# Moving score chunks and mixes among the projections of an attention body

## The reference

```python
q = _split_qk(x @ Wq.T, b, n) * SCALE
k = _split_qk(x @ Wk.T, b, n)
v = (x @ Wv.T).reshape(b, n, H, 2 * D).transpose(0, 2, 1, 3)
att = jnp.einsum('bnqd,bnkd->bnqk', q, k)
att = jax.nn.softmax(att.astype(jnp.float32), axis=-1)
diff = att[:, :, :H, :H] - lam * att[:, :, H:, H:]
out = jnp.einsum('bnah,bhnd->bnad', diff, v)
out = out * jax.lax.rsqrt(jnp.mean(out * out, axis=-1, keepdims=True) + EPS)
out = out * (1.0 - LAM_INIT)
return out.reshape(b, n, DIM) @ Wo.T + bo
```

## Time and profile before

| what | value |
|---|---|
| median of 3 runs | 1276.65 us (1274.16 to 1279.75) |
| the profiled execution | 1274.55 us, its span 1272.7 us |
| TensorE busy | 1100.6 us, 86% |
| VectorE busy | 939.4 us, 74% |
| ScalarE busy | 587.1 us, 46% |
| GpSimd busy | 205.9 us, 16% |
| first `xtl` of body 4 and of body 5 | at 258.81 and 324.28 us |

### The profile page before, as it was taken

How to read it: one execution, slowest core, us unless ns; L and a number is a source line. 1 busy time by engine, 2 the same in 40 slices (tenths; PEclk the granted TensorE clock), 3 DMA queues, 4 the chain that set the end, 5 groups by cost and what they waited for, 6 DMA issues and landing times.

```text
span 1272.7 us, 22077 instructions
## 1 busy us (share of the span) xinstructions
PE 1100.6 (86%) x7424; PEld 873.7 (69%) x7424; DVE 939.4 (74%) x1932; ACT 587.1 (46%) x906; POOL 205.9 (16%) x202
## 2 busy tenths in 40 slices
PE   5988989889797979635599998998989989899995
PEld 4766767667575757424378787787877878778784
DVE  4287878787878888786858677696785867958746
ACT  4333333333243333310346555566555655655683
POOL 3100030303131312132140103003030030210000
PEclk9999999999898989767599999999999999999998
DMA  7566475766657565983530021201211012100001
GB/s 278 158 175 160 140 163 174 157 186 137 200 120 221 100 183 117 290 215 113 193 100 34 1 67 67 66 10 56 66 66 53 13 66 66 66 1 2 34 1 66
DMA packets 184334, 139.32 MB, mean 109 GB/s; under 512 B 140128, under 2 KB 152416, under 8 KB 180192
## 3 DMA queue, kind: packets, MB, share of 16 engines
q1 hardware_dynamic: 113120, 113.57, 31.8%
q10 hardware_dynamic: 71168, 25.17, 8.2%
HBM read 82.09 MB, written 52.43 MB: 106 GB/s over the span
## 4 chain that ended last, share of the span: by engine, by line
PE 66%; DVE 9%; ACT 7%; issue 7%; SPq 5%; DMA 4%; POOL 1%; ACTq 0%; DVEq 0%; POOLq 0%
PE ps_f L558 18%; PE ps_s L744 14%; PE ps_f L728 12%; PE ps_s L577 9%; PE ps_o L679 6%; DMA qbd<-q_scr 3%; SPq L382 3%; PE ps_o L597 2%; ACT h_sb L947 2%; DVE h_acc L1279 1%; ACT r_sb L941 1%; PE ps_t L619 1%; PE ps_f L679 1%; DMA w_raw<-in_L_attn_Wv 1%; ACT oth L919 1%
## 5 line engine op out<-in xcount | busy, mean ns | idle before, releaser
L728 PE MATMUL ps_f<-x2h,w 128*128 128x512 f32 x512 | 204.7, 400 | 1.6 <-DVE x2l L1260 1.6
L744 PE MATMUL ps_s<-w,hh 128*128 128x512 f32 x500 | 201.5, 403 | 0.0
L728 PE MATMUL ps_f<-x2l,w 128*128 128x512 f32 x512 | 200.7, 392 | 0.0
L744 PE MATMUL ps_s<-w,hl 128*128 128x512 f32 x500 | 199.3, 399 | 0.0
L1268 DVE TENSOR_TENSOR hl<-h_sb,hh 128x512 fp32r<-128x512 f32 x128 | 91.1, 712 | 112.2 <-ACT hh L951 110.5
L577 PE MATMUL ps_s<-qbd,k 128*32 128x128 f32 x2048 | 125.4, 412 | 55.0 <-DMA qbd<-q_scr 55.0
L558 PE MATMUL ps_f<-xth,wh 128*128 128x512 f32 x384 | 157.0, 409 | 1.6 <-DVE xtl L1044 1.6
L558 PE MATMUL ps_f<-xth,wl 128*128 128x512 f32 x384 | 150.3, 391 | 0.0
L558 PE MATMUL ps_f<-xtl,wh 128*128 128x512 f32 x384 | 149.8, 390 | 0.0
L577 PEld LDWEIGHTS ps_s<-qbd,k 128*32 128x32 f32 x2048 | 83.4, 149 | 91.9 <-issue 48.7
L1453 POOL TENSOR_TENSOR xb<-xb,bob 128x512 f32<-128x512 f32 x32 | 71.8, 2274 | 434.9 <-DMA xb<-in_x 434.9
(11 more groups left out here) (142 smaller groups left out, 1918.8 us busy)
## 6 DMA issues: line engine op xcount, KB each, us to landing
xa<-in_x SPq DMA_DIRECT2D x8, 1024.0 KB, 5.4
q_scr<-f_sb ACTq DMA_DIRECT2D x32, 256.0 KB, 2.6
k_scr<-f_sb ACTq DMA_DIRECT2D x32, 256.0 KB, 2.8
v_scr<-f_sb ACTq DMA_DIRECT2D x32, 256.0 KB, 5.7
k<-k_scr SPq DMA_DIRECT2D x8, 1024.0 KB, 7.5
qbd<-q_scr SPq DMA_DIRECT2D x128, 64.0 KB, 4.8
w_scr<-w_st SPq DMA_DIRECT2D x32, 256.0 KB, 4.9
v<-v_scr SPq DMA_DIRECT2D x64, 128.0 KB, 6.0
```

Of the source, the lines that this page charges most:

```text
L728: last = nc.tensor.matmul(ps_f[:, j % 2, :], w1[:, k, j * P:(j + 1) * P], xx[:, k, :], start=(k == 0 and xx is x2h), stop=(k == KC - 1 and ...
L744: last = nc.tensor.matmul(ps_s[:, t, :], a[:, j % 4, t * P:(t + 1) * P], w2[:, j, :], start=(j == 0 and a is hh), stop=(j == HC - 1 and a ...
```

## The change

In the TensorE body alone, the order of the pieces is another. Score chunk 0 stood between x transposes 1 and 2, chunk 1 inside projection 0, chunks 2 and 3 behind projections with n = 5 and 7, the mixes behind n = 1 to 4. Now the four x transposes stand together; the chunks stand behind n = 0, 2, 6 and 8 (the 1st, 3rd, 7th and 9th projection) and the mixes behind n = 1, 3, 4 and 5. The hook `beside`, which put chunk 1 inside projection 0, is gone. All other engines keep their order, and no wait is changed.

```diff
@@ -560,7 +560,6 @@
                     if k == KC - 1:
                         last.then_inc(f_ps, 1)
-                    beside(k)
@@ -622,22 +621,16 @@
             def body(i, do_2, do_1):
                 x_transpose(i, 0)
                 x_transpose(i, 1)
-                if do_1:
-                    scores(i - 1, 0, 0, FULL)
                 x_transpose(i, 2)
                 x_transpose(i, 3)
                 if later(i):
                     w_transpose(i - 1, 1, 0)
                 for n in range(12):
-                    def beside(k):
-                        if do_1 and n == 0 and k == 1:
-                            scores(i - 1, 1, 0, FULL)
-
-                    project(i, n, beside)
-                    if do_2 and 1 <= n <= 4:
-                        mix(i - 2, n - 1, 0, G // 4)
-                    if do_1 and n in (5, 7):
-                        scores(i - 1, n // 2, 0, FULL)
+                    project(i, n)
+                    if do_2 and n in (1, 3, 4, 5):
+                        mix(i - 2, max(n - 2, 0), 0, G // 4)
+                    if do_1 and n in (0, 2, 6, 8):
+                        scores(i - 1, (n + 1) // 2 - n // 5, 0, FULL)
```

More of the change, by code:

```diff
@@ L545, in x_transpose, with project @@
                 last.then_inc(xt_ps, 1)
-            def project(i, n, beside):
+            def project(i, n):
                 if n >= 2 or later(i):
```

## The result

The changed kernel takes 1355.14 us (median of 4 runs, 1349.35 to 1357.77) against 1277.54 us before (4 runs): a ratio of 1.0617, 95% interval 1.0593 to 1.0642. It is 6.2% slower. The forecast was 1341.5 us with a range of 1324 to 1362: direction and mechanism came out as forecast, and 14 us of the loss were missing in the sum. The profiled execution took 1355.43 us, its span 1353.6 us. In the rows DVE is VectorE, ACT ScalarE, POOL GpSimd and PE TensorE; each kernel counts its own lines, so the `xtl` of L1044 before is L1037 here.

The account below looks back on a forecast made before the run. TensorE, busy 86% of the span, was taken to lead. Six bodies x (7.2 order + 1.2 + 0.6 clock) plus 10.8 for body 1 made 64.8 us more, 1341.5 us against the 1276.65 median; range 1324 to 1362.

Parts of the forecast that it names:

- This cover is what the change gives away: Body head: chunk 0 (3.9 us) stands largely under the wait for VectorE's late xtl; only 1.1 us is exposed.
- The middle: Before mix 1, TensorE idles 4.2 us for VectorE's turn; in body 1, 5.1 us for ScalarE's queue.
- The late w_in: Before projection 6: w_in lands later, cover 0.6 us, nothing taken; 0.7 us late in body 1, another +7 possible overall.
- The order's sum: Body period at the full clock becomes 72.7 us, 7.2 more: -1.0 earlier projection 0, +3.9 chunk 0, +4.3 stall.
- The clock: After idle gaps at head and middle, projections run at the low clock: 1.2 and 0.6 us a body.
- I take 1.2: Head: projection 0 pays between 0 and 1.8 us for the low clock; 1.2 taken.
- I take 0.6: Middle: projection 4, after the 4.2 us gap, pays 0 to 1.8 us for the low clock; 0.6 taken.
- the worst of one restart: 1.8 us lost by projections to one low-clock restart, from 48 dense matmuls taking 13.18 us against 11.3.
- the sum's own worst case: Both restarts, head and middle, at 1.8 us each on top of 7.2 us a body.
- the upper bound of +77: Whole kernel with every restart at its worst: 6 x (7.2 + 1.8 + 1.8) + 12.6 us.
- slower by more: Rival: clock falls in both gaps and w_in is late, 11.8 us a body, 83 us, 1359 us; 12%.
- The rule of the Trainium skill that the forecast set aside: Head: matmuls should run on while DMA overlaps, so moving chunk 0 behind projection 0 would be a gain.

Follow-up runs that it names:

- signs_early: unstall with the w_in load issued ahead of the second half query load and weight unit 1's signs moved behind the next body's four xtl: 1278.83 us.
- head_only: The kernel before with four x transposes together and score chunks 0 and 1 one behind the other after projection 0: 1321.79 us, ratio 1.0344.
- unstall: The changed kernel with VectorE's soft_first 1 behind mixed_turn 0 and soft_second 0, and ScalarE's exps 1 behind eviction 3: 1342.68 us, ratio 1.0528.
- fill_both: The changed kernel with unused matmuls, 36 between x transposes 1 and 2 and 16 between projection 3 and mix 1: 1331.11 us, ratio 1.0437.
- best_fill2: The best version with unused matmuls, 16 between x transposes 1 and 2 and 5 between transpose 3 and projection 0: 1259.25 us, ratio 0.9890.
- the best version: signs_early with score chunk 1 behind projection 1 in place of 2: 1277.48 us, ratio 1.0008.

## Why the prediction was right, and what its sum lacked

**The head.** Right. "This cover is what the change gives away" was the step that the forecast rested on: `xtl` of tile 0 came late, so chunk 0 ran in time that was idle anyway. The new wait of 9.05 us is released by `xtl`; taking the late `xtl` away (`signs_early`) gave 38 us. `head_only` cost 47.6 us by its own median before, where its expectation had 41, and 12 of them are the wait of mix 1 that it makes.

**The middle.** Right to 0.1 us: 4.19 us before mix 1, forecast 4.2, and in body 1 5.27 us before the projection that waits for ScalarE, forecast 5.1. The late w_in that I allowed for behind the stall, 0.7 us in body 1, made no wait of TensorE there. That ScalarE's order holds the same place and a late w_in stands behind it showed in `unstall`: repairing one of them gave 12 us, both 38.

**The order's sum.** 72.7 us of period at the full clock against 72.6 in `fill_both`. The steps agree too, counted from the first `xtl`: projection 0 starts after 3.6 us (forecast 3.8) and mix 1 after 28.8 (forecast 29.1). So it is not two errors that cancel.

**The clock.** This is the term that was too small: "I take 1.2" at the head and "I take 0.6" in the middle, 1.8 us a body. Measured it is 76.7 - 72.6 = 4.1 us. In body 4 it is 3.3 (75.9 - 72.6), and both places show it. At the head it is 7.5 - 5.7 = 1.8, since the transposes of x and of the weights pay too (1.09 us for four where 0.63 is the full price), not projection 0 alone. In the middle it is 1.5: from mix 1 to mix 2 334.61 - 329.09 = 5.5 us, at the full clock 395.60 - 391.58 = 4.0, and 0.8 of that is mix 1 (1.94 against 1.11), which I had left out. In bodies 3 and 5 it is 8.7 - 5.7 = 3.0 at the head and 6.2 - 4.0 = 2.2 in the middle, more than the 1.8 us that I had called the worst of one restart. I had taken a third of the bound there, for a gap that might or might not be long enough; mix 1 took 1.94 us in each of bodies 2 to 7. The clock's 4.1 us are over the sum's own worst case of 1.8 + 1.8 = 3.6. The 10.9 us a body lie at the sum's worst, 10.8, only because the order cost 6.9 against the mean period before (72.6 - 65.7) and not 7.2. And the loss of 77.6 us lies just above the upper bound of +77: what came true is the first half of the rival "slower by more", to which I gave 12%, the clock low behind both gaps, without its late w_in. The range held the result by the few us that it allowed beyond the bounds. By bodies, the 16.1 us by which the profiled execution exceeds the sum are 3.0 in body 0, 2.4 in body 1, 5 x 1.9 in bodies 2 to 6 and 1.0 in body 7 and behind it.

**What no run settles.** Why the clock fell in body 0 in some executions and not in others, since nothing in the kernel differs there. Part of the scatter of 8 us between runs of the changed kernel may be this.

The rule of the Trainium skill that the forecast set aside ("TensorE: Matmul & The Clock Gate", section "Loop structure matters more than you think") did not decide here: the wait for the query load did go from the heads, as it asks, and `head_only` was 47.6 us slower. In `best_fill2` no head waits for that load either and the kernel is faster than before, but five further edits made that together (the orders of VectorE and ScalarE, the load of w_in, the signs, the place of chunk 1, the unused matmuls), and the rule's own share in it was not tested.

## What to carry to other kernels

Before moving work out of a wait, ask what else ends at about the same time: here a load was named as the releaser, while a second engine was 2 us behind it, and the work moved out of the wait had been nearly free. When an engine's order changes, the fixed orders of the engines beside it become waits: walk each of their queues to the instruction that stands behind the moved one. And price a gap twice, once for its length and once for the clock behind it, by what runs there: here the score chunks took the same time at either clock, while a projection took 5.4 us at the low one against 2.95 and a mix 1.94 against 1.11. Look in the rows for such work before deciding what comes first after a gap.

## What was not expected of the hardware

Giving TensorE 8 us of useless matmuls at the head and 3.6 in the middle made the changed kernel 24 us faster (1355.1 to 1331.1), and 4.7 us of them in each of bodies 2 to 7 made the best version 18 us faster than without. The score chunks, 32 fp32 matmuls with 32 weight columns each, take 3.92 us at a granted clock of 0.50 and of 1.00 alike, while a mix, 16 matmuls of the same shape, took 1.94 against 1.11 us. So two kinds of small fp32 matmul, recorded with the same shape, are priced differently by the clock: at 0.50 both take 0.12 us each, and at 1.00 the mix's take 0.07 and the chunk's still 0.12. What holds the chunk back at the full clock was not tested. One difference stands in the kernel: the moving operand of a score matmul is `qbd[:, :, :, g]`, read with a stride, that of a mix is a slice of `dbd` whose last axis is read whole.
